# New load order at the start, transposes one projection later, and two query projections in one PSUM bank pair

## The reference, cut to what matters

```python
x = L0_attn_hidden_states                       # 1024 tokens, 256 wide
q = (x @ q_proj_w.T)                            # 16 heads of 128 + 64
compressed = x @ kv_a_proj_w.T                  # 64 latent + 64 rotary columns
kv = _rmsnorm(compressed[..., :64], kv_a_ln_w) @ kv_b_proj_w.T
k = concatenate([k_pass, k_rot])                # per head
scores = einsum('bhqd,bhkd->bhqk', q, k) * scaling   # causal, softmax, times v, out projection
```

## Time and profile before

| | us |
|---|---|
| median of 3 runs | 814.84 |
| the runs | 811.56, 814.84, 815.09 |
| the profiled execution, its own time | 816.47 |
| span of the profiled execution | 814.4 |

### The profile page before, as it was taken

One profiled execution on the slowest core, in us unless ns is written; L12 is line 12 of the kernel. 1 busy time (PEld: TensorE's weight loads), 2 busy tenths in 40 slices (PEclk: granted clock), 3 DMA queues, 4 the chain that ended last, 5 costly groups with the idle time before them and its releaser, 6 DMA issues.

```text
span 814.4 us, 16040 instructions
## 1 busy us (share of the span) xinstructions
PE 772.1 (95%) x4643; PEld 652.7 (80%) x4643; DVE 556.0 (68%) x1423; ACT 399.3 (49%) x900; POOL 272.6 (33%) x357
## 2 busy tenths in 40 slices
PE   7999989999989999999989999989999999999997
PEld 7887877767878788777778998888897878888786
DVE  3323778887778778777746666558858387777666
ACT  2224656655656566566514444413333266666531
POOL 2003436434433333322345665624423400000071
PEclk9999999999999999999999999999999999999999
DMA  6349971000000000009339899777622335555431
GB/s 202 112 116 343 404 307 42 35 29 28 22 22 29 15 29 22 14 21 294 112 98 312 282 347 354 255 282 265 257 86 103 129 98 155 155 155 155 110 98 64
DMA packets 49953, 121.26 MB, mean 149 GB/s; under 512 B 7264, under 2 KB 17632, under 8 KB 49760
## 3 DMA queue, kind: packets, MB, share of 16 engines
q1 hardware_dynamic: 38896, 95.94, 35.6%
q0 software_dynamic: 7680, 21.51, 7.4%
q10 hardware_dynamic: 3312, 3.02, 1.1%
HBM read 76.65 MB, written 43.78 MB: 148 GB/s over the span
## 4 chain that ended last, share of the span: by engine, by line
PE 67%; DVE 10%; issue 8%; DMA 6%; POOL 5%; ACT 3%; SPq 1%; DVEq 0%; ACTq 0%; POOLq 0%
PE scores L1624 9%; PE scores L1623 9%; PE scores L1622 9%; PE acc_ps L2034 5%; PE scores L1848 5%; PE misc_ps L1754 4%; PE misc_ps L1752 4%; PE probsT_ps L1739 3%; PE probsT_ps L1761 3%; DMA area<-xe_d 3%; PE acc_ps L1739 2%; DVE xT_lo L1093 2%; PE scores L1858 2%; POOL xd_d L764 2%; DVE neg_max L1087 2%
## 5 line engine op out<-in xcount | busy, mean ns | idle before, releaser
L819 ACT ACTIVATE area<-scores,neg_max 128x128 f32<-128x128 f32 (+7 forms) x128 | 95.0, 743 | 86.7 <-DVE neg_max L1087 85.0
L1087 DVE TENSOR_REDUCE neg_max<-scores 128x1 f32<-128x128 f32 (+7 forms) x128 | 95.7, 750 | 21.8 <-PE scores L1711 21.7
L695 POOL DMA_INDIRECT xe_d<-x_rows,send_i x64 | 64.2, 1003 | 55.4 <-ACT x_rows L843 38.5
L725 POOL DMA_INDIRECT ye_d<-area,home_i x64 | 61.5, 961 | 40.6 <-DVE home_i L1294 19.3
L1848 PE MATMUL scores<-area 128*96 128x128 f32 x512 | 66.7, 273 | 1.4 <-DVE area L1259 0.7
L1622 PE MATMUL scores<-kT_hi,weff_hi 128*128 128x512 f32 (+3 forms) x172 | 66.6, 387 | 0.9 <-ACT area L786 0.4
L683 POOL CAST weff_hi<-area 128x256 fp32r<-128x256 f32 x42 | 17.1, 407 | 135.6 <-PE scores L1711 87.9
L1624 PE MATMUL scores<-kT_hi,weff_lo 128*128 128x512 f32 (+3 forms) x172 | 61.6, 358 | 0.0
L1623 PE MATMUL scores<-kT_lo,weff_hi 128*128 128x512 f32 (+3 forms) x172 | 61.4, 357 | 0.0
L1848 PEld LDWEIGHTS scores<-area 128*96 128x96 f32 x512 | 59.0, 163 | 2.8 <-issue 1.3
L770 POOL DMA_INDIRECT area<-yd_d,slot x16 | 15.7, 981 | 135.7 <-DMA yd_d<-area 131.1
(11 more groups left out here) (292 smaller groups left out, 2041.6 us busy)
## 6 DMA issues: line engine op xcount, KB each, us to landing
area<-w SPq DMA_DIRECT2D x23, 512.0 KB, 4.0
area<-gate_up SPq DMA_DIRECT2D x24, 384.0 KB, 4.7
xe_d<-area SPq DMA_DIRECT2D x8, 1088.0 KB, 12.3
ye_d<-area SPq DMA_DIRECT2D x8, 1024.0 KB, 16.7
area<-w SPq DMA_DIRECT2D x8, 1024.0 KB, 7.4
area<-ye_d SPq DMA_DIRECT2D x15, 512.0 KB, 5.0
area<-xe_d SPq DMA_DIRECT2D x28, 272.0 KB, 6.6
area<-head_w SPq DMA_DIRECT2D x16, 448.0 KB, 3.4
```

What stands on the lines that cost most here:

```text
L695: pool.indirect_dma_start(xe_d, bass.IndirectOffsetOnAxis(send_i[:, t, k:k + 1], 0), x1_rows[:, t, :], None).then_inc(sent[k % 2] if t < T ...
L819: act.activation(row_of(n)[:, 0:L], score_bank(n)[:, 0:L], ACT.Exp, bias=neg_max[:, n % 4:n % 4 + 1], accum_out=rsum[:, s, k:k + 1]).then_ ...
L1087: dve.tensor_reduce(neg_max[:, n % 4:n % 4 + 1], score_bank(n)[:, 0:(n // HEADS + 1) * P], AX.X, ALU.max, negate=True).then_inc(max_ready, 1)
```

## The change

It does five things. SP issues the key weights and the tokens first, then head 0, and waits until the second half of the tokens has landed before it issues head 1 and what follows. PE runs 44 instead of 28 matmuls on the constant, and `absorb(0)` stands between the kv matmuls of token tile 5 and 6 instead of ahead of them; ACT and DVE take head 0's `weff` after the tokens. `transpose_keys(0)` and `(1)` each stand one projection later. Head 1 is projected into `banks[0]`, as head 0 is, after `q_copy` of head 0; the later heads use the pairs the other way round than before. The half of `banks` that is lent moves from the last to the first, and the wait for its last tenant from score tile 65 to 64.

```diff
-IDLE_START = 28
+IDLE_START = 44
...
+        def query_bank(h, u):
+
+            return banks[0] if isinstance(h, int) and h == 0 else banks[1 - u]
...
-        LENT = pT + [acc, half[3]] + half[0:3]
+        LENT = pT + [acc, half[0]] + half[1:4]
...
-                return half[n % AHEAD]
+                return (half[2], half[3], half[1])[n % AHEAD]
...
-            sp.dma_start(heads[:, 0, :], head_w[:, 0, :]).then_inc(ld_head[0], 16)
             sp.dma_start(wkv_a[:].rearrange("p c n -> p (c n)"), wkv_aT).then_inc(ld_kv, 16)
             for b, landed in enumerate((ld_kv, ld_xT)):
                 part = slice(b * BANK, (b + 1) * BANK)
                 sp.dma_start(xT_in[:, :, part], xT.rearrange("(c p) t -> p c t", p=P)[:, :, part]).then_inc(landed, 16)
+            sp.dma_start(heads[:, 0, :], head_w[:, 0, :]).then_inc(ld_head[0], 16)
+            sp.wait_ge(ld_xT, 16)
             sp.dma_start(heads[:, 1, :], head_w[:, 1, :]).then_inc(ld_head[1], 16)
...
-            weff_copy(0, 0)
             round_tokens(0)
             round_tokens(1)
+            weff_copy(0, 0)
...
-            split_weff(0, 0, 0)
             split_tokens(0)
             split_tokens(1)
+            split_weff(0, 0, 0)
...
-                if not (isinstance(h, int) and h < 2):
+                if not (isinstance(h, int) and h < 3):
                     pe.wait_ge(qT_done, h - 1)
+                elif h == 1:
+                    pe.wait_ge(qT_done, 1)
...
-            absorb(0, 0, 0)
             pe.wait_ge(ld_kv, 32)
             for t in range(TILES):
                 if t == TILES // 2:
                     pe.wait_ge(ld_xT, 16)
+                if t == TILES - 2:
+                    absorb(0, 0, 0)
...
-            transpose_keys(0)
             absorb(2, 0, 1)
             project_q(1, 1)
-            transpose_keys(1)
+            transpose_keys(0)
             absorb(3, 1, 1)
             project_q(2, 0)
+            transpose_keys(1)
...
-                if n == SHORT + 1:
+                if n == SHORT:
```

More of the change, by code:

```diff
@@ L785, in q_copy @@
                 hold(act, qT_ps, h + 1)
-                act.activation(qT[:, bass.ds(h * T, T)], banks[u][:], ACT.Copy,
+                act.activation(qT[:, bass.ds(h * T, T)], query_bank(h, u)[:], ACT.Copy,
                                scale=float(QDIM) ** -0.5).then_inc(qT_done, 1)
@@ L1648, in project_q @@
                 pe.wait_ge(weff_split, h + 1)
-                if not (isinstance(h, int) and h < 2):
+                if not (isinstance(h, int) and h < 3):
                     pe.wait_ge(qT_done, h - 1)
+                elif h == 1:
+                    pe.wait_ge(qT_done, 1)
                 for b in range(2):
                     for c in range(HC):
-                        last = product3(banks[u][:, b * BANK:(b + 1) * BANK],
+                        last = product3(query_bank(h, u)[:, b * BANK:(b + 1) * BANK],
                                         (weff_hi[:, u, c, :], weff_lo[:, u, c, :]),
```

## The result

The changed kernel takes 827.7 us (median of 6 runs, 825.62 to 829.84) against 814.97 for the kernel before (6 runs, 811.56 to 824.04): a ratio of 1.017, with a 95% interval of 1.0137 to 1.0204. The forecast was 815.3 us, with a range to 818.2. The profiled execution took 826.68 us, with a span of 824.6, 10.2 us more than the span before (814.4).

What follows compares the result with a forecast made beforehand. PE, busy 95% of the span, was taken as the bound. A start gain of 3.05 us, 3.3 given back and 0.25 for a slower split summed to +0.5 us: 815.3 us, range 811.5 to 818.2.

Steps and rivals of the forecast that it cites:

- the sum: Change in head 3's start: -3.05 gained early, +3.3 given back by new order, +0.25 slower DVE split, total +0.5 us.
- Start of head 1: Head 1's projection start: DVE's keys 3.05 us earlier, and 0.24 us saved by the transposes' absence ahead of it.
- I take 14.4, near the middle: DVE's key start, held by the landing of `x_in`: 14.4 us against 17.45 before, a gain of 3.05 us.
- the late bound of 15.8: Latest landing of `x_in`, if the load queue runs dry and the tokens land at their late bound.
- the forecast's longest case: Tokens' second half to `x_in` with the queue run dry: at most 2.7 us on top of 5.0.
- Ahead of head 2: Wait for `split_weff(2)` behind `split_keys(0)` after the transposes: 1.7 us new, plus 0.25 for POOL's split beside it.
- Head 2 to head 3: Head 2's projection 2.93, then `split_keys(1)` and `wvo_copy(1)` 0.69 + 2.00, then 0.40 us to head 3.
- rival 3: Clock falls again at PE's new standstills near the start: 2.4 us per fall, two give 820.1 us; chance 0.08.
- the 1.4 us wait before left the pace alone: Argument against rival 3: behind the earlier wait, 12 projection matmuls still took 2.94 us, 0.245 each.
- rival 1: Start's gain goes through with new waits hidden: 811.8 us, or 810.3 if the keys' wait is filled too; chance 0.10.
- rival 2: Head 0's query copy binds head 1's start if head 1's weights land at 13.1: 816.3 us; chance 0.10.
- rival 4: Tokens land no earlier, since the first load's start sets the time: +4.1 us, 818.9 us; chance 0.06.

Runs made afterwards that it cites:

- experiment 2: Changed kernel with both key transposes back in their old places, one projection earlier, SP's wait kept: 821.81 us, ratio 1.0083.
- experiment 4: Changed kernel with 44 idle matmuls filling PE's standstill behind head 0's projection: 820.98 us, ratio 1.006.
- experiment 12: Reordered DVE list with the attention's first pauses filled, and SP's wait for the tokens put back: 816.16 us, ratio 1.0017.
- experiment 1: Changed kernel without SP's wait for the tokens ahead of head 1's load: 824.45 us, ratio 1.0133.
- experiment 7: Changed kernel without SP's wait, late transposes kept, DVE's list put in the order PE now asks for: 817.61 us, ratio 1.003.
- experiment 6: Kernel before with the change's query banks, lent seats and score halves alone: 815.69 us, ratio 1.0004.
- experiment 10: Kernel before with 68 idle matmuls ahead of head 3's absorption, to start the attention later: 819.51 us, ratio 1.0038.
- experiment 11: Kernel before with 7, 3 and 11 idle matmuls in the attention's first three pauses: 818.98 us, ratio 1.0043.
- experiment 3: Changed kernel without SP's wait and with the transposes in their old places: 818.17 us, ratio 1.0025.
- experiment 9: Changed kernel without SP's wait, DVE's list reordered, plus 7, 3 and 11 idle matmuls in the attention's first three pauses: 811.25 us, ratio 0.9967.

## Why the prediction was wrong

The mechanisms that the sum named all came. Two steps failed: one term, the landing of `x_in`, was mis-sized, and the sum took every projection at full pace, with the half clock behind a standstill only among the rivals. From the traces of before and after, head 3's start moved by +5.79 us (28.53 to 34.32), in four pieces:

- **Start of head 1: -0.48** (20.32 to 19.84), forecast -3.05 - 0.24 = -3.3. The tokens and the pace were right (first half about 5.0 against 6.0 forecast, kv end 10.94 against 10.4). The step that failed is the landing: "I take 14.4, near the middle". `x_in` landed at 16.85, 1.05 us beyond even the late bound of 15.8, and the keys started at 16.91. The second half of the tokens came at 7.79, and then 9.06 us passed to `x_in`, where the forecast's longest case has 2.7 + 5.0 = 7.7. The queue did run dry behind the wait, for about as long as that case allows (3 us from 6.75), but a second low followed that the forecast didn't have: 91 to 179 GB/s from 10.5 to 12.75, whose cause was not traced. The time from the second half to the keys repeats, 9.1 us here and 9.2 to 9.3 in experiments 2, 4 and 12, which keep the wait. The 7.79 doesn't: there the second half came at 6.62, 6.39 and 6.77, and the keys started at 15.95, 15.63 and 15.99, still later than forecast. "Head 2's load queues behind it, but `absorb(2)` waits for later things" was right only in part: that load held the first matmuls of `absorb(2)` to 17.91, which made the long standstill, while the last one waited for DVE's copy, done at 19.13, which set head 1's start. From there to head 1 it took 0.71 us and not 0.40, since the clock was already down. Experiment 1 moves the keys from 16.91 to 14.20 by taking the wait away.
- **Head 1's projection: +2.32** (5.26 for 2.94), forecast 0. This is the first fall of the clock, and the term that the sum lacked.
- **Ahead of head 2: +2.19** (3.32 for 1.13, from the transposes on), forecast 1.7 + 0.25. Right, and the wait is the one named, `split_weff(2)` behind `split_keys(0)`.
- **Head 2 to head 3: +1.76** (5.90 for 4.14), forecast 1.88 (6.02 for 4.14). Right, though the wait for the copy itself was 1.13 us and not 1.9. Experiment 7 shows both by taking them away: with DVE's list in the new order, head 3 starts at 23.50.

Behind head 3 come +1.6 us to the first row maximum (the second fall; 48.1 us for 46.5), +1.7 in the attention (the third), and 1.1 later. So of the 10.2 us, 0.5 was the forecast, 2.5 is the late landing, 0.3 + 2.3 + 1.6 + 1.7 = 5.9 the clock, 0.1 the waits' sizes, and 1.1 lies behind the attention and wasn't traced further.

The judgement behind the missing term is that of rival 3. Its price per fall (2.4 us) was fair, but it got a chance of 0.08 and two falls at most, and "the 1.4 us wait before left the pace alone" was carried over to pauses it doesn't cover: 2.67 us in one piece, 1.84, and 1.13 with 0.32 close before. Experiment 4 shows that the clock falls behind the first of them and that it doesn't when the pause is filled. The Trainium skill's warning of idle gaps between bursts ("TensorE: Matmul & The Clock Gate", section "HAM oscillation") was named beside the rival, and the traces agree with it: 0.51 from 18 to 25 us behind 2.67 us of waiting. Rivals 1, 2 and 4 did not occur: head 0's copy ends at 16.38, 1.5 us ahead of `absorb(2)`.

One thing in the baseline was not typical either. Head 0's projection starts at 14.62 in the profile of before, but at 13.11, 13.36 and 12.56 in experiments 6, 10 and 11, whose start is that of before. So a common execution of before gives the new load order 1.3 to 2 us less to win than the rows did; with 73.5 and 73.0 for the first row maximum in experiments 6 and 11, experiment 3's 71.7 is a lead of 1.3 to 1.8, and the 1.5 us that its attention takes longer (317.0) use it up. By these profiles, one for each kernel, that is why it stands level with before.

## What to carry to other kernels

Where PE is the bound, a pause costs its length and can cost half clock behind it. At this kernel's start, waits of 2.67, 2.84 and 3.64 us were each followed by it (the change, experiments 12 and 2). Of three waits of 1.84 us two were, in experiments 1 and 4; of two of 1.71 us one, in experiment 1; of six of 1.39 to 1.42 us none. Waits of 0.32 and 1.13 us close together were followed by it in the change, and 0.26 and 1.09 us in experiment 1 were not. So a fall behind a new pause is a term with a price and a chance, not a remote rival; and where the pause can't be avoided, work, even idle matmuls, can be put into it (experiment 4); where no fall was, filling gained nothing (experiment 11). When steps are moved on one engine, move them in the lists of the engines that feed it too: with DVE's list unchanged, the new order made two waits that the same calls in another order remove. A wait in a load queue lets the queue run dry, here to 24 to 94 GB/s for 3 us, and every load behind it is late; ask which of them is needed first.

## What was not expected of the hardware

- The same rows at the attention's start, with the same pauses of 0.43 and 0.69 us, bring the clock down in some kernels and not in others. With the pauses unfilled it did not fall where the first row maximum came at 73.5, 75.0, 75.2, 75.5 and 77.1 us, and fell where it came at 70.0, 71.7, 72.0, 78.7, 78.9 and 82.4. One profile stands for each kernel; what decides it was not found, and experiment 10 missed the place that would have tried it.
- Half-clock stretches of 3.4 to 6.8 us also stand between 530 and 550 or 605 and 622 us in the profiles of nine of the twelve experiments, and in neither that of before nor that of after; experiment 9 has one at 419 to 422. Each costs up to half its length, about as much as the effects that were to be measured: in experiments 2, 7 and 11 what follows the attention takes 428.1, 427.6 and 429.3 us in place of 423.9. They are not the whole of that spread: without one in those places the same part takes 420.4 us in experiment 6 and 425.0 after the change. Which kernel gets one was not settled. Part of experiment 9's lead over before is a fuller clock, but only part: over all runs beside each other its mean lies 0.0017 above that of before, worth 1.4 of 4.6 us by the same estimate.
- The granted clock can't be read alone at the start. Before, it shows 1.00 while the kv matmuls run at the lower pace; in experiments 6 and 10 it shows 0.50 from 8 to 10 us for the same matmuls.
